# Routing a mixture of experts batch by batch, and moving half of its row scatters from one stage into the stage before it

## What is computed

```python
# attention: Q, K, V of 16 heads of 16; 64 landmarks: means over 32 tokens
kernel1 = softmax(Q @ K_l.T); kernel2 = softmax(Q_l @ K_l.T); kernel3 = softmax(Q_l @ K.T)
SV = (kernel1 @ iterative_inv(kernel2)) @ (kernel3 @ V)       # iterative_inv: 6 iterations on 64x64
out = SV @ w_proj
# experts: 16 experts in 4 groups, 2 groups and then 4 experts for each token
scores = sigmoid(x2d @ router_weight.T)
sc = scores + e_bias
gidx = top_k(sum(top_k(sc per group, 2)), 2)
tidx = top_k(where(group chosen, sc, 0), 4)
tw = scores[tidx] / sum(scores[tidx]) * 2.5
routed = sum over the 4 experts of tw * (silu(x @ gate.T) * (x @ up.T)) @ down.T
out = routed + shared
```

## Time and profile before

| | us |
|---|---|
| median of 3 runs | 2089.93 |
| lowest, highest | 2079.41, 2092.99 |
| profiled execution: span | 2087.8 |

### The profile page before, as it was taken

How to read it: one execution, slowest core, us unless ns; L and a number is a source line. 1 busy time by engine, 2 the same in 40 slices (tenths; PEclk the granted TensorE clock), 3 DMA queues, 4 the chain that set the end, 5 groups by cost and what they waited for, 6 DMA issues and landing times. The chain is left out here.

```text
span 2087.8 us, 34165 instructions
## 1 busy us (share of the span) xinstructions
PE 1792.3 (86%) x11999; PEld 946.9 (45%) x11999; DVE 1506.7 (72%) x3496; ACT 1008.5 (48%) x1908; POOL 537.1 (26%) x592
## 2 busy tenths in 40 slices
PE   0898937899999999999999789797247888999998
PEld 0565612232323333333332356465146556888854
DVE  7997559898989999999999481685036894444456
ACT  3464413566767777777768453463002454332210
POOL 0343261000000000001320000102723884666610
PEclk9999968899999999999999899898568999999999
DMA  3457574022120413232611441003214323655556
GB/s 101 146 192 237 192 178 82 1 68 90 55 103 33 125 50 109 72 86 91 187 52 42 169 172 51 1 2 108 105 41 136 128 96 110 188 189 188 167 207 224
DMA packets 158713, 238.69 MB, mean 114 GB/s; under 512 B 19762, under 2 KB 127282, under 8 KB 156882
## 3 DMA queue, kind: packets, MB, share of 16 engines
q1 hardware_dynamic: 122706, 152.46, 24.5%
q0 software_dynamic: 23136, 75.65, 10.2%
q10 hardware_dynamic: 12704, 8.39, 1.2%
HBM read 116.23 MB, written 119.82 MB: 113 GB/s over the span
## 5 line engine op out<-in xcount | busy, mean ns | idle before, releaser
L1118 ACT ACTIVATE c_prob<-c_pst 128x512 f32<-128x512 f32 (+1 forms) x1152 | 579.7, 579 | 297.9 <-PE c_pst L1079 173.0
L1226 DVE TENSOR_REDUCE c_mx<-c_pf 128x2 f32<-128x1024 f32 x384 | 459.7, 1222 | 33.1 <-PE c_pf L1060 29.5
L1079 PE MATMUL c_pst<-c_qa,c_ka 128*128 128x512 bf16 (+3 forms) x1280 | 362.6, 358 | 8.2 <-DMA c_qa<-c_mT 4.8
L1095 PE MATMUL c_po<-c_prob,c_vh 128*32 128x512 f32 (+3 forms) x2560 | 294.1, 541 | 0.3 <-issue 0.3
L1060 PE MATMUL c_pf<-c_ka,c_qa 64*128 64x512 bf16 (+3 forms) x1280 | 230.0, 366 | 47.5 <-DMA c_ka<-s_kbias 22.6
L1222 DVE CUSTOM_DVE_ANT_0 c_spare<-c_pf,c_cut 128x384 f32<-128x384 f32 (+3 forms) x512 | 231.0, 492 | 28.7 <-PE c_pf L1060 24.3
L1079 PEld LDWEIGHTS c_pst<-c_qa,c_ka 128*128 128x128 bf16 x1280 | 110.4, 97 | 203.7 <-ACT c_prob L1118 113.4
L1060 PEld LDWEIGHTS c_pf<-c_ka,c_qa 64*128 64x128 bf16 x1280 | 59.3, 93 | 311.1 <-DVE c_mx L1226 121.5
L992 POOL IOTA c_zero<- 128x24 int32 x6 | 1.3, 214 | 631.2 <-PE c_po L1095 631.2
L2047 POOL DMA_INDIRECT s_parts<-x_yr,x_tags x144 | 140.8, 978 | 86.1 <-DVE x_yr L2702 62.7
L2586 PE MATMUL x_ps<-x_gu,x_xs 128*128 x576 | 138.0, 383 | 0.0
(11 more groups left out here) (383 smaller groups left out, 2916.1 us busy)
## 6 DMA issues: line engine op xcount, KB each, us to landing
s_slots<-c_zero POOLq DMA_DIRECT2D x6, 3264.0 KB, 16.9
x_xr<-s_slots SPq DMA_DIRECT2D x72, 272.0 KB
x_rows<-s_parts SPq DMA_DIRECT2D x8, 2048.0 KB, 8.8
c_qa<-s_qs SPq DMA_DIRECT2D x64, 192.0 KB, 7.6
c_ka<-s_ks SPq DMA_DIRECT2D x64, 192.0 KB, 8.3
s_qs<-b_parts SPq DMA_DIRECT2D x32, 256.0 KB, 2.4
s_ks<-b_parts SPq DMA_DIRECT2D x32, 256.0 KB, 2.7
s_vs<-b_va SPq DMA_DIRECT2D x32, 256.0 KB, 3.7
```

Source lines behind the costliest of these rows:

```text
L1079: mm = nc.tensor.matmul(pst[:, u % NS, at:at + qn], ka[:, s, hh, kt * P:(kt + 1) * P], qa[:, s, hh, qb * QB + q0:qb * QB + q0 + qn], start ...
L1095: mm = nc.tensor.matmul(po[HV * h:HV * h + HV, q0:q0 + qn], vh[:, s, kt, h, :], prob[:, a % NP, h, at:at + qn], start=(kt == 0), stop=(a i ...
L1118: nc.scalar.activation(prob[:, g % NP, hh, 0:w], pst[:, u % NS, 0:w], ACT.Exp).then_inc(exp_ok, 1)
L1226: nc.vector.tensor_reduce(mx[:, fh:fh + 2, qt, part], pf[:, slot, :, 0:kn], AX.X, ALU.max).then_inc(max_ok, 1)
```

## The change

The routing code becomes a class `Routing`, used once for each batch (16 token tiles of 128 instead of 32), with the same operations on half as many elements.

- `join_and_project`: a first Sigmoid over batch 0's logits at i = 5, ahead of that step's other work on ScalarE; TensorE's two count matmuls for batch 0 behind the products of i = 7; VectorE's `route(0..3)` at i = 5 to 8, which routes batch 0 as far as place and share of choice 0. GpSimd prepares the constants here (eight instructions that stood in the next stage), SyncE loads `e_bias` here. Logits take two PSUM banks instead of one.
- `landmarks_and_kernel3`: `route(n)` finds choices 1 to 3 of batch 0 (n = 0 to 2), then routes batch 1: group scores (3), groups (4), ranks with four experts a step (5 to 8), pick (9), weights (10), counts at COUNT = 11, slots (11, 12), choices 0 to 2 (13 to 15). SyncE loads batch 0's rows four tiles at a time into two buffers. GpSimd sends batch 0's 64 scatters as 16 quartets; before each quartet it waits for all scatters so far to land, writes two tags, and for choice k waits for `place_ok`. The two GpSimd multiplications for the inverse come behind the seventh quartet. The stage ends after the last scatter has landed.
- `inverse`: no scatters. SyncE loads batch 1's 16 tiles twice, GpSimd tags both copies. VectorE finds choice 3 of batch 1 (half size) at iteration 0, compares owners at 1 (over 32 ends, where it was 16), finds owners at 2 (the same, and two more small operations).
- `kernel1`: batch 1's 64 scatters, two a tile as before; tags of choices 2 and 3 are written at tile 16 and 24, 16 columns each.
- Slots: batch 1's pairs first fill what batch 0 left free in each expert's last tile, so that the number of slot tiles is unchanged.

```diff
@@ join_and_project, ScalarE
+            def first_probabilities(_):
+                act.wait_ge(l_ok, NCH)
+                nc.scalar.activation(prob[:, 0:NB]..., pl[:, 0, 0:NB * E], ACT.Sigmoid).then_inc(prob_ok, 1)
-            in_turn([(2, NCH, root(1)), (0, N, take), ...
+            in_turn([(2, NCH, root(1)), (NCH + 1, 1, first_probabilities), (0, N, take), ...
@@ TensorE
+            in_turn([(0, N, turn), (1, N, products), (N - 1, 1, counts)])
@@ VectorE
+            def route(m):
+                if m == 0:
+                    dve.wait_ge(prob_ok, 1)
+                    router.group_scores(); router.choose_groups(); router.count_experts(range(0, 4, 2))
+                elif m == 1:
+                    router.count_experts(range(4, E, 2)); router.pick(picked_ok)
+                elif m == 2:
+                    router.weights()
+                else:
+                    dve.wait_ge(counted, 1)
+                    router.take_counts(below_counts, all_counts)
+                    ...
+                    router.place_and_share(0, slot_of[:, 0, 0:NB], share[:, 0, 0:NB])
+            in_turn([..., (1, NCH, sum_up), (NCH + 1, 4, route)])
@@ landmarks_and_kernel3, SyncE
-            sp.dma_start(eb[:], e_bias...)
+            for g in range(NR // RG):
+                if g >= 2:
+                    sp.wait_ge(sent, 16 * (g - 1) * RG * TOPK)
+                sp.dma_start(send_rows[:, g % 2, :, 0:C], rows_dram...[:, g * RG:(g + 1) * RG, :]).then_inc(send_in[g % 2], 16)
@@ GpSimd
+            def tag(g, k):
+                done = (g * TOPK + k) * RG
+                wait(pool, sent, 16 * done)
+                wait(pool, place_ok, k)
+                step(nc.gpsimd.iota(send_rows[:, g % 2]...[:, :, C:C + 1], ...))
+                step(nc.gpsimd.tensor_copy(send_rows[:, g % 2, :, C + 1:C + 2], tiles(share[:, k], g)...))
+                if k == 0:
+                    pool.wait_ge(send_in[g % 2], 16 * (g // 2 + 1))
+            def send(g, k):
+                for i in range(RG):
+                    scatter(nc, slots_dram, place[:, k, g * RG + i:...], send_rows[:, g % 2, i, :]).then_inc(sent, 16)
+            for n in range(NPR):
+                g, k = divmod(n, TOPK)
+                tag(g, k)
+                send(g, k)
+                if n == 6:
+                    marks_done()
+            pool.wait_ge(sent, 16 * NR * TOPK)
@@ inverse, GpSimd
-                for t in range(min(NR, early - k * NR)):
-                    ...
-                    scatter(nc, slots_dram, place[:, k, t:t + 1], xrows[:, t, :]).then_inc(sent, 16)
-            pool.wait_ge(sent, 16 * early)
@@ inverse, VectorE
-                if it + 1 < TOPK:
-                    find_place_and_share(it + 1)
-                elif it + 1 == TOPK:
+                if it == 0:
+                    find_place_and_share(TOPK - 1)
+                elif it == 1:
                     compare_owners()
-                elif it == TOPK:
+                elif it == 2:
                     find_owners()
```

More of the change, by code:

```diff
@@ L1905, in chosen @@
-            def chosen(n, top):
-                both(tt, rank[:, 0, :, 0:n], rank[:, 0, :, 0:n], rank[:, 1, :, 0:n], ALU.add)
-                both(ts, rank[:, 1, :, 0:n], rank[:, 0, :, 0:n], float(top), None, ALU.is_lt)
-            def choose_groups():
-                start_ranks(GR)
-                count(gs[:], GR, range(0, GR, 2))
-                chosen(GR, TOPG)
-                both(tt, groups, groups, rank[:, 1, :, 0:GR].unsqueeze(3).to_broadcast([P, NR, GR, EG]), ALU.mult)
-                start_ranks(E)
@@ L1932, in _ @@
-            turned = lambda a: a.rearrange("p t e -> p e t")
+            lanes = Lanes(dve, chain, 2)
+            routers = [Routing(nc, lanes, comb[:, b * NR:(b + 1) * NR], route_of["rank"][b],
+                               route_of["places"][b], route_of["picked"][b], work, consts, b, route_of["top"], route_of["scale"])
+                       for b in range(2)]
             def take_counts(n, bm, r):
@@ new lines, in take_counts, with find @@
+                    dve.sem_inc(taken, 1)
+            def find(b, k):
+                routers[b].place_and_share(k, place[:, k, b * NR:(b + 1) * NR], share[:, k, b * NR:(b + 1) * NR])
+            def route(n, bm, r):
+                second = routers[1]
+                if n < TOPK - 1:
+                    find(0, n + 1)
+                    dve.sem_inc(place_ok, 1)
+                elif n == TOPK - 1:
+                    second.group_scores()
+                elif n == TOPK:
+                    second.choose_groups()
+                elif n < TOPK + 1 + E // 4:
+                    i = 4 * (n - TOPK - 1)
+                    second.count_experts(range(i, i + 4, 2))
+                elif n == TOPK + 1 + E // 4:
+                    second.pick(picked_ok)
+                elif n == TOPK + 2 + E // 4:
+                    second.weights()
@@ L2048, in scatter, with inverse @@
                                         in_offset=None)
-def inverse(nc, KTb, Vb, VTb, tbd, W, comb, rank, ends, ahead, place, share, owner, rows_dram, xrows, slots_dram, early, TOPK, NPR, ITERS,
-            ctx):
+def inverse(nc, KTb, Vb, VTb, tbd, W, comb, route_of, place, share, owner, rows_dram, xrows, TOPK, NPR, ITERS, ctx):
     sb = lambda name, shape, dt=F32: ctx.enter_context(nc.sbuf_tensor(name, shape, dt))
@@ L2085, in inverse @@
         sem(f"i_{n}") for n in ("id0", "eye_ok", "mm_ok", "dv_ok", "ac_ok", "w_ok"))
-    rows_in = [sem(f"r_rows_in{i}") for i in range(2)]
+    rows_in = sem("r_rows_in")
     with nc.Block() as block:
@@ L2340, in _ @@
             staggered(pool, N, DEPTH, [(0, send), (3, normalise)])
-            wait(pool, sent, 16 * (TOPK * NR - early))
+            for i in range(2):
+                pool.wait_ge(sent[i], 16 * TOPK // 2 * NR)
         @block.tensor
@@ L2795, in two_layers @@
                         comb = s2("comb", [P, N // P, E])
[L2796 to L2799 removed]
+                        NB = N // P // B
+                        both = range(B)
+                        bf = lambda name, shape: k23.enter_context(nc.sbuf_tensor(name, shape, BF16))
+                        consts = dict(eb=s2("r_eb", [P, E]), keep=s2("r_keep", [P, E, NB]), steps=s2("r_steps", [P, NB]),
+                                      one_e=s2("r_one_e", [P, E]), below=bf("r_below", [P, P]), ones=bf("r_ones", [P, P]))
+                        ends, free, first_ = s2("r_ends", [P, B * E]), s2("r_free", [P, E]), s2("r_first", [P, E])
+                        rank, slots_ahead = s2("r_rank", [P, B, 2, NB, E]), s2("r_ahead", [P, B, E, NB])
+                        picked = bf("r_picked", [P, B, NB, E])
+                        route_of = dict(groups=GROUPS, top=(TOP_GROUPS, TOP_K), scale=SCALE, rank=[rank[:, b] for b in both],
+                                        picked=[picked[:, b] for b in both],
+                                        places=[dict(ahead=slots_ahead[:, b], ends=ends, free=free, first=first_) for b in both])
                         tbd = s2("tbd", [P, NPR, 32])
```

433 lines of the change are left out of this document (249 added, 184 removed).

## The result

The kernel after takes 2025.8 us (median of 4 runs, 2022.5 to 2036.0), the kernel before in the same comparison 2090.4 (4 runs). The ratio is 0.971 with a 95% interval of 0.968 to 0.975: faster, by 65 us. The forecast was 2015, its range 2000 to 2068.

What follows compares the result with a forecast made beforehand. Bound by stage, chiefly TensorE; the inverse was stalled by GpSimd's back-to-back scatters. -83.5 + 2 (clock) + 2 (join) + 6 (kernel 3) - 1.5 (kernel1) = -75 from 2087.8, plus 2.1 for the median: 2015 us, range 2000 to 2068.

Steps and rivals of the forecast that it cites:

- Inverse: Inverse without scatters: gain 83.5 us, from 78.6 for the stalled window and 5 for half its edges; 2 lost to clock.
- zero, with 3 us either way: Inverse: VectorE's changed routing would hold TensorE up about 12 us, where it was 11.8.
- The 2 us for a low clock at the stage's start: Inverse: first products may run at the lower clock because kernel 3's end leaves TensorE idle; 2 us lost.
- Join: Join: batch 0's routing stays hidden on VectorE; table load, count matmuls and a load issue add 2 us, bounds 0 and +4.
- Kernel 3: Kernel 3: TensorE and VectorE unchanged (-3 to +3); GpSimd's scatters end the stage 6 us later, bounds 0 and +31.
- The rule against it: Kernel 3: the skill page's shared-port lock would delay more than the one scatter in six priced at 5 us.
- A: Rival, kernel 3: the port lock or slower landings hold most scatters, so GpSimd ends late; 2040 us, chance 0.10.
- Kernel1: Kernel1: tags ready beforehand and no wait for landed rows save 1.5 us, bounds -3 and 0.
- B: Rival, kernel 3: TensorE runs at half speed under the scatters and loses 40 us; 2049 us, chance 0.14.
- D: Rival, kernel 3: the stall lasts through the quartets' rests, costing 105 us; slower, 2120 us, chance 0.07.
- C: Rival: full stall under kernel 3's quartets, 2090 us, or the inverse stalls for another reason, about 2096; chance 0.09.
- under 8 a us: Kernel 3: sign that the forecast is wrong, TensorE's pace falling below 8 matmuls a us.

Runs made afterwards that it cites:

- e1: Kernel before, with the inverse's 64 scatters sent in kernel1 instead; inverse 75.9 us, kernel1 236.4 us.
- e3: Kernel after, with GpSimd sending kernel 3's scatters only after the last tile of pairs; VectorE's last division at 143.2 us (140.4 before, 154.4 after).
- e6: Kernel before, with a GpSimd memset of 128x320 behind each scatter of the inverse; inverse 122.1 us.
- e4: Kernel after, with GpSimd's two multiplications apart, behind the third and fifth quartets instead of both behind the seventh; kernel 3 took 151.0 us.
- e5: Kernel after, with a row load per quartet in kernel 3, each quartet waiting only for the last but one to land; kernel 3 took 174.7 us.
- e8: e1 plus 64 plain GpSimd DMAs of whole rows, no index, in the inverse, to an array nothing reads; inverse 72.9 us.
- e2: Kernel before, with the inverse's scatters waiting after every four until all so far have landed; inverse 126.8 us.
- e9: Kernel before, with a one-column GpSimd memset behind each scatter of the inverse; inverse 140.6 us.
- e7: e1 plus 64 indirect GpSimd DMAs in the inverse, 64 bytes of each row, to an array nothing reads; inverse 154.8 us.

## Why the prediction was right, and where it was off

*Inverse (-83.5 and +2; measured -86).* The cause held: e1 takes the scatters away and 78.8 us go. That is the lower bound, the stalled window alone; the half of the edges wasn't there to be gained. The step that was off is the routing, "zero, with 3 us either way": it gave 7.3 us (75.9 to 68.6). I had the hold-ups themselves about right: 12.2 us of TensorE's waiting for VectorE, where "about 12" stood. What I left out is that a hold-up mostly costs the next product its clock as well, and that three hold-ups do so less often than five. The 2 us for a low clock at the stage's start had no ground: its first window after the change has PEclk 1.00.

*Join (+2; measured +1.7 and +1.1).* As worked out. VectorE's routing is 117 operations and 27.9 us where 118 and 31 were counted, and its wait ahead of the last landmarks product is still there. Routing operations by stage, join and kernel 3 (as the earlier trace rows):

```profile
1174.00:1300.70 126.70, 27.87 (x117) 0.93 0.45 157
1300.80:1455.40 154.60, 40.28 (x147) 0.92 0.21 72
```

VectorE at the join's end (timeline, as the earlier trace rows):

```profile
1299.40 0.49 DVE L1642 TENSOR_SCALAR QL<-e_pq 128x128 f32<-128x128 f32 x2 [5.67 <-PE e_pq L1533]
```

*Kernel 3 (+6; measured +14 and +18.5).* This is the step that failed. "0 (-3..+3)" for TensorE and VectorE and +6 for GpSimd's end: the second was right to 1 us (landed 1446.5, forecast 1447), the first was not. The second was right in part by luck: as written, 1348 + 92 + 2.3 gives 1442.3 and not 1443.5, and only with 1442.3 does the 5 us of collisions lead to 1447; the fourth quartet started a microsecond early, and the quartets were 7.6 us apart in the mean (the one with the multiplications corrected for their 2.3 us) instead of 7.1. The first was put at nothing. Its parts, from the first profile: +3 from the routing (e3), where I wrote "the count step is shorter by 1" and the slots' step had grown to 13 operations (all the routing there took 40.3 us in 147 operations, where "about 35" stood); +5.4 at the pair of multiplications, which I had priced as GpSimd's time only (3.8 us) and not as VectorE's; and the rest, about 5.5, in pauses by scatters back to back (6.3 us of such waits on VectorE, not all on the path) and in the clock behind them. These pauses don't stand still. In the second profile the stage has 4.5 us more: its first tile runs at the lower clock (5.40 us for 8 matmuls instead of 3.70), and a pause comes ahead of tile 10. The first profile has its own pause of 2.9 us behind the last tile, so that from there to the end it takes 20.0 us, and the second 15.5.

*The rule against it.* I had looked for the collision between VectorE's operations and the scatters, and priced it at 5 us: 64 scatters took 64.9 us in sum, 1014 ns each, where 967 was the median of before, so 3 us. The rows show which scatters are hit. In the earlier trace rows VectorE's operation ends at 1475.55 and the scatter that began inside it at 1476.40, 0.85 us later. The longest of all runs is in e6 (timelines of VectorE and GpSimd):

```profile
1494.32 2.54 DVE L57 TENSOR_TENSOR r_before<-r_ends,r_tiles_f 1x2304 f32<-1x2304 f32 x1
1495.17 2.54 POOL L2047 DMA_INDIRECT s_slots<-x_rows,place  x1 [0.28 <-POOL i_fill L2126]
```

1496.86 and 1497.71, again 0.85 us. Both operations of VectorE have both inputs in SBUF. Over all runs, in kernel 3 and the inverse, 59 scatters begin inside such an operation (at least 0.05 us behind its start and 0.15 us ahead of its end), and all of them end 0.77 to 0.92 us after it. 26 that begin in the same way inside one with an input in PSUM, and 102 inside a reduction, take 0.95 to 1.11 us as ever. In kernel 3 of the kernel after it was 6 of 64, beside operations of 0.2 to 0.7 us; so little was lost, and A didn't come. In the prediction I let the page's wait of descriptors hold for an operation with two inputs in SBUF. The Trainium skill, SBUF — State Buffer, section "Who interferes with whom", has GpSimd's descriptors wait behind VectorE's two-port modes and takes `tensor_tensor` out of it. For an indirect DMA these rows show otherwise, and they decide.

The collision that cost was between two computing instructions. The operation that lasts 4.36 us reads two inputs in SBUF against a GpSimd operation that reads SBUF. The Trainium skill, SBUF — State Buffer, section "SBUF: two separate sides", says of just this pair that whichever starts first gets the shared ports for the whole instruction. The ends agree: in both profiles of the kernel after and in e4 VectorE's operation ends with the multiplication it met (4.36, 4.37, 1.48 and 0.74 us). The starts agree only in e4; in the kernel after, as recorded, VectorE's operation starts first, by 0.56 and 0.58 us, and still waits. The rule was at hand, and I applied it to one of GpSimd's instructions where it bears on others as well.

*Kernel1 (-1.5; measured +0.9 and +1.2).* The gain of 1.5 us isn't there. The experts differ by 3.3 us between two profiles of one kernel, so I read nothing into it.

*The rivals.* A: quartets were mostly 7.1 to 8.4 us apart, not 9. B and D: TensorE's pace between pauses stayed at 6.7 us a tile, and the clock over kernel 3 is 0.92. Yet B's mechanism is real: it moved with the scatters and cost some 5 us in the first profile, and more in the second, where B had 40; and e5 shows how near the edge this was: rests of 0.9 us instead of 2.3, and 20 us more are gone. C fell with e1. D's point, 81 us lost in kernel 3, was never near.

*The signs.* Those for the inverse and the join came: one piece of "issue" (2.8 us, at the stage's start, as in e1), a stage of 68.6 us, VectorE idle for 5.67 us ahead of the last landmarks product. Those for kernel 3 did not. Its last instruction is no scatter; TensorE shows 2.8 us of "issue" before `t_p`; and from 1370 to 1420 us it does 350 matmuls, 7.0 a us, 293 in the 50 us from 1373 in the second profile, where 407 stood before. By my own sign, "under 8 a us", the forecast was wrong for this stage, though the time fell into its range.

*The sum.* 2015 against 2025.8. Of the 11 us, by the second profile, kernel 3 makes 12.5, kernel1 2.7 and what lies ahead of layer 1 1.6; the inverse takes 5.0 back, the join and the experts 1.7. That the forecast met the first profile's span so closely says nothing of its terms: two profiles of the kernel after lie 10 us apart.

## What to carry to other kernels

When TensorE shows single matmuls with "issue" before them, look at whether GpSimd sends indirect DMAs back to back, and try some 0.7 us between them before moving anything: one memset behind each scatter (e6, one run) took the inverse from 154.7 to 122.1 us, half of what the whole change brought, and left the structure as it was. When an instruction of GpSimd is moved, ask what on VectorE runs beside it in the new place: beside a reduction of PSUM the multiplications cost nothing, and an operation with two inputs in SBUF waited until they had ended. And count behind a hold-up of TensorE a slower product (here behind six of eight).

## What the runs showed of the hardware

| GpSimd's DMAs in the inverse | start to start, us | "issue" on TensorE, us | TensorE's work ends |
|---|---|---|---|
| none (e1) | | 3.0 | 75.1 |
| 64 plain, 139 KB each (e8) | 0.53 | 2.8 | 71.8 |
| 64 indirect, 139 KB, a memset between (e6) | 1.71 | 4.0 | 84.9 |
| 64 indirect, quartets, landing awaited (e2) | 1.27 and 2.7 | 19.3 | 95.6 |
| 64 indirect, one column between (e9) | 1.41 | 48.8 | 139.9 |
| 64 indirect, back to back (before) | 1.32 | 68.3 | 153.9 |
| 64 indirect, 8 KB each (e7) | 1.27 | 68.1 | 153.8 |

Indirect DMAs of GpSimd that follow each other closely hold up TensorE's issuing, with 8 KB each as with 139, and the effect is steep: from 1.71 to 1.41 us between starts it goes from nearly nothing to 49 us. Of the stages seen here the inverse, with its dense stream of small matmuls (17 a us), suffered most: quartets cost it 20 us of 76 (e2), and kernel 3 (8 a us) some 5 to 10 of 141. Whether it is the rate or the size of the matmuls no run parts.

What connects the two is not settled. The profile lists a DMA queue of the kind "instruction" (q8), which by its name brings instructions to the engines. In 75 us of e7's stall it has no transfer, in 73 us of e1 it has ten. The DMA view of e7, 1465 to 1540 us:

```profile
q0 software_dynamic: 1888, 0.49, 3.2%
```

and of e1, 1440 to 1513 us:

```profile
q1 hardware_dynamic: 4038, 4.10, 16.3%
q8 instruction: 10, 0.16, 0.9%
```

But a TensorE that issues one matmul a microsecond uses up few instructions, so this can be the stall's effect as well as its cause, and no run here parts the two; it would take the same matmuls in a loop that needs no new instructions.
